# Attention scores in three rotating PSUM banks, and the head outputs turned back by narrow products

## The reference, cut to what matters

```python
# layer 1, first attention ("self" in the kernel): causal, q and k normed by head
q, k, v = x_n @ Wq.T, x_n @ Wk.T, x_n @ Wv.T
q, k = layernorm_by_head(q) * gq + bq, layernorm_by_head(k) * gk + bk
x = x + softmax(q @ k.T * scale + causal_mask) @ v @ Wo.T + bo
# layer 1, second attention ("local"): queries x_n, keys and values from the context, |i - j| <= 64
x = x + softmax(x_n @ ctx.T * scale + window_mask) @ ctx @ W_proj.T + b_proj
# then a linear layer on block-quantised activations, added to x
```

## Time and profile before

| | |
|---|---|
| median of 3 runs | 1455.29 us (1454.81 to 1456.36) |
| the profiled execution's own time | 1459.37 us, its span 1457.6 us |
| busy in the span | PE 89%, DVE 74%, ACT 72%, POOL 43% |
| granted TensorE clock, mean | 0.972 |

### The profile page before, as it was taken

How to read it: one execution, slowest core, us unless ns; L and a number is a source line. 1 busy time by engine, 2 the same in 40 slices (tenths; PEclk the granted TensorE clock), 3 DMA queues, 4 the chain that set the end, 5 groups by cost and what they waited for, 6 DMA issues and landing times.

```text
span 1457.6 us, 42538 instructions
## 1 busy us (share of the span) xinstructions
PE 1294.8 (89%) x15257; PEld 942.1 (65%) x15257; DVE 1081.9 (74%) x2573; ACT 1049.3 (72%) x2841; POOL 633.9 (43%) x844
## 2 busy tenths in 40 slices
PE   4358999999999999999984999889889989999995
PEld 1125676666666666767674999856656666676664
DVE  6998889999899988876665344466668778686665
ACT  2128999999999999999981566647666766766653
POOL 0012424353444434310215554448675776655663
PEclk9999999999999999999995999979999999999997
DMA  6942242413214241020112332220101010000000
GB/s 145 242 121 57 52 102 53 113 49 95 66 48 100 52 108 49 16 94 2 52 35 66 101 96 75 96 84 22 32 10 42 11 41 11 26 25 4 25 11 16
DMA packets 83579, 89.00 MB, mean 61 GB/s; under 512 B 15792, under 2 KB 72752, under 8 KB 78768
## 3 DMA queue, kind: packets, MB, share of 16 engines
q1 hardware_dynamic: 77424, 77.10, 20.3%
q0 software_dynamic: 4096, 8.40, 2.0%
q10 hardware_dynamic: 1856, 0.79, 0.2%
HBM read 64.76 MB, written 17.83 MB: 57 GB/s over the span
## 4 chain that ended last, share of the span: by engine, by line
PE 60%; DVE 13%; ACT 10%; issue 8%; POOL 5%; DMA 2%; ACTq 0%; another core or an unknown queue 0%; DVEq 0%; SPq 0%; POOLq 0%
PE P L796 7%; PE P L958 7%; PE P L2114 5%; PE P L1579 4%; PE P L1612 4%; PE P L814 3%; PE P L940 3%; ACT pr L1019 3%; PE P L917 3%; PE P L928 3%; PE P L912 3%; PE P L2176 2%; PE P L2132 2%; PE P L835 2%; PE P L2069 2%
## 5 line engine op out<-in xcount | busy, mean ns | idle before, releaser
L2433 DVE TENSOR_REDUCE mx<-P 128x8 f32<-128x1024 f32 x128 | 156.5, 1223 | 123.8 <-PE P L2114 85.3
L1019 ACT ACTIVATE pr<-P,nm 128x256 f32<-128x256 f32 x512 | 238.6, 499 | 5.9 <-DVE nm L1217 5.7
L2326 ACT ACTIVATE et<-P 128x1024 f32<-128x1024 f32 x128 | 131.0, 1024 | 122.6 <-PE P L2121 110.2
L1217 DVE TENSOR_REDUCE nm<-P 128x4 f32<-128x1024 f32 x128 | 156.1, 1219 | 25.9 <-PE P L796 23.5
L796 PE MATMUL P<-kt_w,qt 64*128 64x256 f32 x1024 | 145.2, 402 | 4.6 <-ACT pr L1019 4.6
L1001 ACT COPY ptS<-P 128x512 f32<-128x512 f32 x256 | 138.1, 598 | 8.7 <-PE P L814 8.4
L992 ACT ACTIVATE pr<-pr,ri 128x256 f32<-128x256 f32 x254 | 119.6, 536 | 24.6 <-DVE pr L1190 24.0
L704 POOL TENSOR_TENSOR kv_qk<-kv_qk,mixing 128x512 f32<-128x512 f32 x48 | 61.0, 1271 | 151.9 <-DVE pr L1190 151.9
L1675 ACT ACTIVATE hT<-P,mixing 128x128 f32<-128x128 f32 x284 | 81.0, 368 | 61.1 <-PE P L1579 56.8
L698 POOL TENSOR_TENSOR kv_qk<-kv_qk,r_w 128x512 f32<-128x512 f32 x48 | 61.0, 1270 | 145.6 <-DVE pr L1190 100.0
L1019 ACT ACTIVATION_READ_ACCUMULATOR pr<-P,nm 128x1 f32 x512 | 118.2, 231 | 0.0
(11 more groups left out here) (351 smaller groups left out, 3652.4 us busy)
## 6 DMA issues: line engine op xcount, KB each, us to landing
kv_qk<-scr_v SPq DMA_DIRECT2D x16, 1024.0 KB, 8.0
r_w<-scr_r SPq DMA_DIRECT2D x16, 1024.0 KB, 10.8
xt<-scr_xs SPq DMA_DIRECT2D x71, 64.0 KB, 1.8
scr_ys<-yt SPq DMA_DIRECT2D x71, 64.0 KB
x<-in_x SPq DMA_DIRECT2D x8, 256.0 KB, 10.2
scr_v<-mixing SPq DMA_DIRECT2D x8, 256.0 KB, 2.5
scr_r<-mixing SPq DMA_DIRECT2D x8, 256.0 KB, 2.0
xb<-in_x SPq DMA_DIRECT2D x8, 256.0 KB, 3.3
```

Of the source, the lines that this page charges most:

```text
L1019: e = nc.scalar.activation(pr[:, s % 3, h * KEYS:(h + 1) * KEYS], scores(s)[:, h // 2, (h % 2) * KEYS:(h % 2 + 1) * KEYS], ACT.Exp, bias=n ...
L1217: nc.vector.tensor_reduce(nm[:, s % 3, 0:4].rearrange("p (a h) -> p a h", a=2), scores(s).rearrange("p a (h k) -> p a h k", k=KEYS), AX.X, ...
L2326: nc.scalar.activation(et[:, u % 4, :, :, :], scoresT, ACT.Exp).then_inc(S["h_exp"], 1)
L2433: nc.vector.tensor_reduce(mx[:, n % 2, 8 * r:8 * r + 8].rearrange("p (k a) -> p k a", k=2), scores, AX.X, ALU.max, negate=True).then_inc(S ...
```

## The change

1. The scores of a unit's two quarters go to two of the three banks 0, 1 and 6 in turn: half-unit 2s+k uses bank number (2s+k) mod 3 of that list. A mask of half-unit i waits for the maximum of half-unit i-3 only. DVE takes the maximum by two instructions, of one bank each.
2. Bank 6 is no longer `turned`. The turning back is now a plain f32 product of `ot` with 36 columns of the unit matrix (9 of each 32) in place of a transpose with all 128, and its 144 columns lie in bank 4 beside `wo_bank`. The output product L2223 moves ahead of the turning back in the slot, DVE's addition moves to just behind the division, and waits keep the two uses of bank 4 apart.
3. The q and k products are two steps `qk0` and `qk1` of two matmuls each, into bank 7 as `products`; ACT copies 512 columns at once (twice) rather than 256 (four times). `qp` of group 1 goes the same way. `v` moves later by four slots in groups 2 and 3. Some more steps are in `MIDDLE`.
4. The maxima are turned in the middle of the next even slot's scores, behind head a = 1, instead of at the end of the odd slot.

```diff
-    ... "qk0": -24, "qk1": -23, "qk2": -22, "qk3": -21, ...
+    ... "qk0": -23, "qk1": -21, ...
-MIDDLE = (("qt0", 1), ("kt3", 1), ("qt3", 1), ("kt1", 2), ...
+MIDDLE = (("qk0", 1), ("kt3", 2), *[(_name, _g) for _name in ("kt2", "qt1") for _g in range(4, GROUPS - 1)], ("qt0", 1), ...
...
-            scores = P[:, 0:2, :].rearrange("p k (m n) -> p k m n", m=4)
+            SCORE_BANKS = (0, 1, 6)
-            qk_bank = P[:, 4, 2 * T:4 * T]
-            turned = P[:, 6, :]
+            turned = P[:, 4, T:T + H * (DH + 1)]
+            def score_bank(s, k):
+                return P[:, SCORE_BANKS[(2 * s + k) % 3], :]
+            def half(s, k):
+                return 2 * s + k + 1
...
+                def products(s, middle):
+                    for k in range(2):
+                        g = self_at(s, f"qk{k}")
+                        if g and ((f"qk{k}", g) in MIDDLE) == middle:
+                            bank7_free(f"qk{k}", g)
+                            pe.wait_ge(S["h7_read"], filled("dxt", g))
+                            for i in range(2):
+                                b = 2 * k + i
+                                m = nc.tensor.matmul(bank7[:, 256 * i:256 * i + 256], xTd[:, b * T:(b + 1) * T], wD[:, 0:256], ...)
+                            m.then_inc(S["h7"], 1)
...
-                        if s:
-                            pe.wait_ge(S["h_max"], s)
                         for k in range(2):
-                            nc.tensor.matmul(P[:, k, :], identb[:, :], bcast(maskb[:, local, :], 1, 4),
+                            if half(s, k) > 3:
+                                pe.wait_ge(S["h_max"], half(s, k) - 3)
+                            nc.tensor.matmul(score_bank(s, k), identb[:, :], bcast(maskb[:, local, :], 1, 4),
                                              start=True, stop=False)
...
+                        if a == 1 and s % 2 == 0:
+                            maxima(s // 2 - 1)
...
+                    # output product, moved ahead of the turning back
+                    if 0 <= u < UNITS_H and u % 2:
+                        n = pass_of(u)
+                        pe.wait_ge(S["h_oth"], n + 1)
+                        if n:
+                            pe.wait_ge(S["h_add"], n)
+                        if u + 1 < UNITS_H:
+                            pe.wait_ge(S["h_on"], n + 1)
+                        nc.tensor.matmul(wo_bank, oTh[:, n % 2, :], ...)
...
                         if u >= 2 and u % 2 == 0:
                             pe.wait_ge(S["h_on"], u // 2)
+                            if adds_until(s):
+                                pe.wait_ge(S["h_add"], adds_until(s))
                         for t in range(2):
-                            m = nc.tensor.transpose(turned...[:, t, u % 2], ot[:, u % 2, t, :], ident[:, :])
+                            m = nc.tensor.matmul(turned...[:, t, u % 2], ot[:, u % 2, t, :],
+                                                 ident[:, :].rearrange("p (a j x) -> p a j x", a=2, j=2)[:, :, :, 0:DH + 1],
+                                                 start=True, stop=True)
...
-                    if s % 2:
-                        maxima(s // 2)
...
-                        nc.vector.tensor_reduce(mx[...8 * r:8 * r + 8]..., scores, AX.X, ALU.max, negate=True)...
+                        for k in range(2):
+                            nc.vector.tensor_reduce(mx[...8 * r + 4 * k:8 * r + 4 * k + 4],
+                                                    score_bank(s, k)..., AX.X, ALU.max, negate=True).then_inc(S["h_max"], 1)
```

More of the change, by code:

```diff
@@ L105 @@
         "sum0": 2, "sum1": 2, "sum2": 6, "sum3": 7, "stat0": 8, "stat1": 8, "nm": 9, "xn0": 9, "xn1": 10,
[1 row of a table removed]
+        "dxt": 11, "bias": 11, "qk0": 13, "qk1": 15, "square": 15, "v": 17, "reduce": 16,
         "guess": 17, "inv0": 18, "inv1": 19, "kn": 20, "qn": 21,
@@ L110 @@
         "sum0": 12, "sum1": 14, "sum2": 19, "sum3": 20, "stat0": 14, "stat1": 20, "nm": 21, "xn0": 21, "xn1": 22,
[1 row of a table removed]
+        "dxt": 23, "bias": 23, "qk0": 25, "qk1": 27, "square": 27, "v": 29, "reduce": 28, "guess": 29,
         "inv0": 30, "inv1": 31, "kn": 34, "qn": 35,
         "kt0": 35, "qt0": 36, "kt1": 37, "qt1": 38, "kt2": 39, "kt3": 40, "qt2": 41, "qt3": 42},
-    4: {**{f"gather{k}": 17 + k for k in range(2 * GS)}, "sum0": 23, "sum1": 24, "stat0": 29},
+    4: {**{f"gather{k}": 17 + k for k in range(2 * GS)}, "sum0": 23, "sum1": 24, "stat0": 29, "qk0": 33, "qk1": 34},
     5: {"sum0": 35, "sum1": 40},
@@ L2113, in score @@
                         cols, part = slice(b * T, (b + 1) * T), slice(64 * r + 32 * k, 64 * r + 32 * k + 32)
-                        return nc.tensor.matmul(scores[:, k, a, :], q[part, a, cols], keys[part, a, cols], start=False,
+                        return nc.tensor.matmul(score_bank(u, k)[:, a * T:(a + 1) * T], q[part, a, cols], keys[part, a, cols], start=False,
                                                 stop=(a == 3))
@@ L2179, in tensor_program @@
                         m.then_inc(S["h_pv"], 1)
[L2182 to L2190, removed]
-                                             stop=True).then_inc(S["qk"], 1)
+                    u = s - 8
+                    if 0 <= u < UNITS_H and u % 2:
[5 more added lines that the diff above has]
+                            pe.wait_ge(S["h_on"], n + 1)
+                        nc.tensor.matmul(wo_bank, oTh[:, n % 2, :], (wE if unit(u)[0] else wDo)[:, :], start=True,
+                                         stop=True).then_inc(S["h_wo"], 1)
                     u = s - 6
@@ L2214, in tensor_program @@
                         nc.tensor.transpose(oT_bank, on3[:, n % 2, :], ident[:, :]).then_inc(S["h_tr"], 1)
[L2215 to L2235 removed]
+                    products(s, False)
                     g = self_at(s, "v")
@@ L2300, in operands, with products @@
                                                  scale=gbs[:, 6:7]).then_inc(S["h7_read"], 1)
+                def products(s, middle):
+                    for k in range(2):
+                        g = self_at(s, f"qk{k}")
+                        if g and ((f"qk{k}", g) in MIDDLE) == middle:
+                            got(f"qk{k}", g)
+                            if k == 0:
+                                act.wait_ge(S["d_qkn"], 2 * (g - 1))
+                            nc.scalar.copy(qkv[:, g % 2, 2 * k:2 * k + 2, :].rearrange("p b n -> p (b n)"), bank7)\
+                              .then_inc(S["h7_read"], 1)
                 for s in range(FIRST_H, LAST_H):
@@ L2344, in scalar_program @@
                           .then_inc(S["h_ot"], 1)
[L2346 to L2361 removed]
+                    turned_rows(s, False)
+                    products(s, False)
                     g = self_at(s, "v")
```

105 lines of the change are left out of this document (34 added, 71 removed), and 6 rows, old and new, of tables (SELF, SELF_BY_SLOT).

## The result

The changed kernel takes 1474.22 us (median of 4 runs, 1471.13 to 1476.17), the kernel before 1455.82 in the same comparison: ratio 1.0126, 95% interval 1.0111 to 1.0141. It is 18.4 us slower, where the forecast was 4.7. Sign and range held, the size did not.

What follows compares the result with a forecast made beforehand. PE was taken as the bound, with idle time from a loop through the maximum. 368.4 of passes and 64.2 of steps made 432.6; 16 of waits made 448.6, +4.7 on 443.9, so 1460.0 us, range 1444 to 1477.

Steps and rivals of the forecast that it cites:

- Rival A: Third phase: PE's own work takes the place of the loop; 1460 us, own range 1454 to 1468, chance 0.58.
- rival C: Odd slot's scores: the DMA of the maxima becomes the new loop; 1475 us, chance 0.13.
- Turning back +0.22 a slot: Turning back in each slot: four product records replace two transposes, +0.22 us a slot, 26 us in 120 slots.
- D: Turning back: the narrow product pays by its columns, 0.32 us a slot less than taken; 1432 us, chance 0.05.
- Maxima amid the scores +0.30: Even slot's scores: the maxima's transpose put in their midst costs PE +0.30 us a pass, 18 us in 60 passes.
- Half maxima 1.3: DVE: two half maxima take 1.3 us where one took 1.22, hidden in DVE's idle time.
- B: Third phase: the waits go too, with 3 to 4 us of them remaining; 1447 us, chance 0.24.
- What holds it is a loop through the maximum: Pass without steps: masks wait for the maximum, 3.07 us even and 3.34 odd, leaving PE 1.01 us idle.
- 60 x 6.14: Slots 8 to 127: 60 passes of 6.14 us of PE work each, 368.4 us.
- steps of 64.2: Slots 8 to 127: PE's work on fills and `qk` steps for other groups, 64.2 us in all.
- "16" of remaining waits: Slots 8 to 127: 10 us of waits kept, plus 2 each for bank 7, DMAs and low clock: 16 us.
- its median is 4.1 lower: Whole kernel: profiled execution would reach 1464.1 us, and the median lies 4.1 lower, at 1460.0 us.

Runs made afterwards that it cites:

- e1: Changed kernel with the turning back as two transposes by an identity with permuted columns, instead of the 36-column products: 1459.03 us.
- e3: Kernel before with only the turning back changed, to plain products of nine columns per head into bank 6: 1467.47 us, ratio 1.0088.
- e4: Kernel before with only the transpose of the maxima moved amid the next even slot's scores: 1465.16 us, ratio 1.0071.
- e5: Changed kernel with the transpose of the maxima moved between the even slot's second mask and first score: 1459.01 us.
- e8: Changed kernel with parts 1, 2 and 4 undone, leaving product pairs, fills amid the slot and the output product's new place: 1455.05 us, ratio 0.9999.
- e2: Changed kernel with the transpose of the maxima back at the odd slot's end: 1465.45 us, ratio to the kernel before 1.0080.
- e7: Changed kernel with score halves in two banks, 0 and 1, instead of three: 1476.99 us, ratio to the kernel before 1.0143.
- e6: Changed kernel with both permuted-identity transposes for the turning back and the maxima's transpose between masks and scores: 1446.65 us, ratio to the kernel before 0.9937.
- e11: The kernel of e6 with output product and turning back ahead of the values' products in each slot: 1450.85 us, ratio to the kernel before 0.9974.

## Why the prediction was right in sign and short in size

*The mechanism, right.* Rival A, that PE's own work takes the loop's place, is what e1, e3, e4 and e5 show. But A's own range of 1454 to 1468 did not hold 1474.22. The stated range held it only because it reached up to rival C, whose number of 1475 is nearly the measured one and whose mechanism did not occur; that is luck. A bare pass of 6.14 was forecast and is 6.13; one with two fills 7.02, and is 3.67 + 3.37 = 7.04. The masks wait 0.6 us in the stretch. Turning back +0.22 a slot: the rows above give 0.47 - 0.28 and 0.69 - 0.50, 0.19 each, and e1's bare slots 0.24 and 0.14. Its records are 0.11 apart for 36 columns as for 128, but for one of four in odd slots (0.03), so D fell. Maxima amid the scores +0.30: 0.41 less 0.11. Half maxima 1.3: 1.37, hidden. The wait for `qk` went, and bank 7 gave it back; e8 measures the sum as zero. C, the DMA as a new loop: the waits of PE in the stretch have none for it. B fell, since the waits that remain were not under 11.3 us.

*One reading of the mechanism, wrong.* "What holds it is a loop through the maximum" is so for the even slot of 3.07. The 3.34 of a bare odd slot were held by the other loop, mostly: L2105 started 0.14 us behind the end of ACT's copy to `ot`, when the maximum had been ready for 0.27, whereas it starts 0.06 behind a maximum that comes last. The time did go away in a bare pass, as part 4 moves L2105 to a place where the copy is long done, so the 6.14 came out right; but it is no gain of the third bank, as e2's 3.33 shows.

*The sum, wrong by 13.7 us* (4.7 forecast, 18.4 measured). Three terms and a slip:

1. *"60 x 6.14".* The window of 443.9 us that I compared with ends at the start of slot 127, so it holds 119 slots and not 120. With 59.5 passes of 6.13 the term is 364.7 and not 368.4, 3.7 lower. The slip hid part of the other errors.
2. *"steps of 64.2".* I priced each fill at 0.44 and two products at twice that, from rows where they stand at the slot's end behind their like. By the slots' medians the steps add 72.9 us: 49 single fills in even slots x 0.43, 22 in odd ones x 0.48, six even slots with two fills x 1.43, eight odd slots with a pair of products and a fill x 1.61, and 18 more slots with 19.8 together. (One of the 18, slot 34, took 7.99 us with a wait of 3.3 for POOL; it is counted here at the 0.95 of a pair of products in an odd slot, and its other 3.8 fall to the waits of term 3.) So 8.7 too low. By these numbers the six even slots with two fills have the largest share, 6 x (1.43 - 0.88) = 3.3, and the eight with a pair and a fill 8 x (1.61 - 1.32) = 2.3. The excess is in fills amid the slot (0.59), in a pair or a step of eight records, which takes 0.97 or 0.98 and not 0.88, and in the second fill of a slot, which often waits for ACT.
3. *"16" of remaining waits.* 455.0 - 59.5 x 6.13 - 72.9 = 17.4: 1.4 too low.

So far 8.7 + 1.4 - 3.7 = 6.4 in the stretch, and 0.7 outside it: behind slot 127 38.4 us instead of the 36.9 of before (I wrote 36.7) that I left unchanged, ahead of slot 8 0.8 less. That makes 11.8 between the two profiled executions (1459.37 and 1471.13) against 4.7.

4. *"its median is 4.1 lower".* I moved the profiled difference onto the median as if the other kernel's profile would lie as high. It is the lowest of its four runs, 3.1 below their median, and that of before is 3.6 above its own: 6.6 us more. One execution of a kernel can lie anywhere in some 10 us (before: 1449.4 to 1460.1). e7's stretch is 5.6 longer than the changed kernel's with every kind of slot of the table the same; 4.7 of it are in three slots (34, 61 and 62). e8, with a median equal to before, has a profiled stretch 6.9 shorter, as its profiled execution lies 2.2 under its median and that of before 3.6 above. 5.9 of the 6.9 are in even slots; how much of that is chance, and how much comes of the `qk` steps that left them, one profile of each can't tell.

*What the forecast did not see at all* is that the costs were of order and place. 0.30 for the insertion was priced right and accepted. The same record costs 0.10 ahead of the first score (e5), and a permuted identity gives 36 packed columns at a transpose's price (e1); the 27.6 us of e6 are in these two.

Open: which of the executions' varying waits make up the 6.6 us was not traced, as each kernel has one profile. In e6 values' products still wait 10.1 us for POOL's select; e11 halves that, at a price that is higher.

## What to carry to other kernels

Before freeing an engine of a wait, count how many passes really pay for it: a loop's idle time that other steps fill is worth nothing, and any work added to the engine then counts in full. On PE, price a small operation by the shapes of its neighbours, and try it next to records of its own shape first. Take the length of a kernel from medians, and differences between single profiles only slot by slot, by the median of slots of one kind, or by their shortest where they scatter. And read who ended each wait before naming the loop: two loops can end within some 0.2 us of each other, and the change may open only one.

## What the hardware showed that was not expected

- An f32 product with 36 moving columns paces like one with 128: four records in 0.47 us, 0.11 apart. In the odd slots of the changed kernel, behind L2208, the second record followed the first by 0.03, and four took 0.36. As a transpose the same takes two records, 0.28 and 0.22 in these two places.
- A transpose takes a permuted identity, and gives its columns in that order at the same pace (0.22 for two in e1). Written 36 columns apart, each over the junk of the one before, four fit in 236 columns instead of 512.
- One full-height transpose costs 0.41 us amid row-tiled products of 32 rows, 0.11 between full-height ones and 0.10 between masks and scores; two cost 0.37 between row-tiled and 32-wide products against 0.28 behind 32-wide ones (products with v, 32 weight columns each).
- Of DVE's maximum of 1024 f32 columns (1.22 us) a half takes 0.685, so splitting costs 0.15.
